# A new order of the work ahead of the loop in a gated cross-attention kernel, with the SiLU table loaded by an instruction of its own

## What is computed

```
x = x + tanh(g_xattn[0]) * L0_xattn(layernorm(x), ctx)      # softmax(q k^T) applied to x
x = x + tanh(g_ffn[0])   * L0_ffn(layernorm(x))             # 256 -> 2 x 704 -> 256
x = x + tanh(g_xattn[1]) * L1_xattn(layernorm(x), ctx)      # 16 heads of 128
x = x + tanh(g_ffn[1])   * L1_ffn(layernorm(x))             # 64 experts, top 8, and a shared one
```

```
def bit_linear(x, w, g):                       # activations to 8 bits, weights to -1, 0, 1
    xn = x * rsqrt(mean(x * x) + 1e-5) * g
    s = 127 / max(|xn|);   xq = round(xn * s) / s
    return xq @ wq.T
gate, up = split(bit_linear(x, gate_w, g1))
return bit_linear(gate * sigmoid(gate) * up, down_w, g2)
```

## Time and profile before

| | |
|---|---|
| median of 3 runs | 617.92 us (616.35 to 618.05) |
| profiled execution | 618.08 us |
| its span in the trace | 616.3 us |
| PE busy | 603.2 us (98%), 3637 matmuls |
| DVE busy | 479.2 us (78%) |
| ACT busy | 422.3 us (69%) |
| POOL busy | 236.1 us (38%); eight to nine tenths in slices 2 to 7 of 40, six or less behind them |
| granted clock of PE | nine tenths or more of full speed in all 40 slices |

### The profile page before, as it was taken

How to read it: one execution, slowest core, us unless ns; L and a number is a source line. 1 busy time by engine, 2 the same in 40 slices (tenths; PEclk the granted TensorE clock), 3 DMA queues, 4 the chain that set the end, 5 groups by cost and what they waited for, 6 DMA issues and landing times.

```text
span 616.3 us, 11599 instructions
## 1 busy us (share of the span) xinstructions
PE 603.2 (98%) x3637; PEld 523.1 (85%) x3637; DVE 479.2 (78%) x1139; ACT 422.3 (69%) x1080; POOL 236.1 (38%) x280
## 2 busy tenths in 40 slices
PE   8889999999999999999999999999999999999997
PEld 6657899999999999999998888888887888887886
DVE  4899889887778687688775787788777677777776
ACT  6998999888888888889898344465444444443442
POOL 5989898666665666556662020000000000000000
PEclk9999999999999999999999999999999999999999
DMA  8423211000000000000030545452956466544540
GB/s 295 147 78 103 82 49 49 31 1 3 1 2 2 2 2 2 1 2 1 11 120 2 157 153 161 128 165 88 226 156 168 116 173 174 157 153 149 196 128 34
DMA packets 33654, 56.47 MB, mean 92 GB/s; under 512 B 12801, under 2 KB 13505, under 8 KB 33601
## 3 DMA queue, kind: packets, MB, share of 16 engines
q1 hardware_dynamic: 33312, 55.82, 29.9%
q10 hardware_dynamic: 288, 0.00, 0.0%
HBM read 53.45 MB, written 1.31 MB: 89 GB/s over the span
## 4 chain that ended last, share of the span: by engine, by line
PE 85%; POOL 4%; DVE 4%; issue 3%; ACT 3%; DMA 1%; SPq 0%; DVEq 0%; ACTq 0%; POOLq 0%
PE bank L298 24%; PE bank L300 24%; PE bank L299 24%; PE bank L967 4%; PE bank L942 2%; PE bank L934 2%; POOL att L584 1%; PE bank L887 1%; DMA wqk<-in_qk 1%; ACT w L1457 1%; PE bank L867 1%; PE bank L814 1%; PE bank L1008 1%; PE bank L801 1%; POOL rk L566 1%
## 5 line engine op out<-in xcount | busy, mean ns | idle before, releaser
L1603 ACT ACTIVATE inter_hi<-inter 128x512 fp32r<-128x512 f32 x63 | 39.8, 632 | 140.6 <-DVE inter L2266 140.6
L298 PE MATMUL bank<-xnT_hi,front_hi 128*128 128x512 f32 (+1 forms) x260 | 102.0, 392 | 0.0
L300 PE MATMUL bank<-xnT_hi,front_lo 128*128 128x512 f32 (+1 forms) x260 | 101.8, 391 | 0.0
L299 PE MATMUL bank<-xnT_lo,front_hi 128*128 128x512 f32 (+1 forms) x260 | 101.7, 391 | 0.0
L2270 DVE TENSOR_TENSOR inter_lo<-inter,inter_hi 128x512 fp32r<-128x512 f32 x63 | 43.6, 692 | 37.9 <-ACT inter_hi L1603 37.3
L1555 ACT ACTIVATE att<-bank,shift,rq 128x256 f32<-128x256 f32 x128 | 71.4, 573 | 0.3 <-DVE shift L2156 0.2
L584 POOL TENSOR_TENSOR att<-att,rowinv 128x512 f32<-128x512 f32 x60 | 63.5, 1074 | 10.6 <-DVE rowinv L2166 10.4
L2239 DVE TENSOR_TENSOR prod<-gate_s,bank 128x512 f32<-128x512 f32 x63 | 43.3, 687 | 21.8 <-PE bank L300 19.7
L566 POOL TENSOR_TENSOR rk<-msq,minus_half 128x4 f32<-128x4 f32 x32 | 33.1, 1035 | 67.9 <-DVE msq L2138 67.7
L2149 DVE TENSOR_REDUCE rowmax<-bank 128x2 f32<-128x512 f32 x64 | 43.7, 685 | 19.2 <-PE bank L300 18.9
L300 PEld LDWEIGHTS bank<-xnT_hi,front_lo 128*128 128x128 f32 x260 | 48.8, 188 | 11.4
(11 more groups left out here) (272 smaller groups left out, 1814.6 us busy)
## 6 DMA issues: line engine op xcount, KB each, us to landing
w_all<-w_rows SPq DMA_DIRECT2D x128, 128.0 KB, 3.0
raw<-in_expert_w SPq DMA_DIRECT2D x32, 384.0 KB, 3.6
wvo_raw<-in_expert_w SPq DMA_DIRECT2D x16, 384.0 KB, 3.6
e_more<-in_expert_w SPq DMA_DIRECT2D x16, 384.0 KB, 3.6
raw<-in_head_qk SPq DMA_DIRECT2D x8, 384.0 KB, 3.7
wvo_raw<-in_head_vo SPq DMA_DIRECT2D x4, 384.0 KB, 3.1
w_keep<-in_head_vo SPq DMA_DIRECT2D x4, 384.0 KB, 3.3
gate_raw<-in_gate_wT SPq DMA_DIRECT2D x2, 704.0 KB, 9.0
```

Source lines behind the costliest of these rows:

```text
L298: pe.matmul(out, l_hi, r_hi_, start=start, stop=False, skip_group_check=True)
L299: pe.matmul(out, l_hi, r_lo_, start=False, stop=False, skip_group_check=True)
L300: return pe.matmul(out, l_lo, r_hi_, start=False, stop=stop, skip_group_check=True)
L1603: act.activation(inter_hi[:, slot, :], inter[:, slot, :], ACT.Copy).then_inc(a_Ihi, 1)
```

## The change

The four lists ahead of the loop are replaced: the same calls stand in them in another order and in part with other PSUM banks, and the bare waits between PE's calls follow the banks. Not only the order differs:

- `load_table(ACT.Silu)` stands directly ahead of `silu_0(0)`, and no longer behind `copy_q2(1, 4)`.
- PE's `keep_busy(1, 7)` became `keep_busy(3, 7)`, and `keep_busy(0, 4)` is new ahead of `gate_0(4)`.

The functions that the lists call, the loop and everything behind it are the same. The core of the diff, with most of the four lists left out (DVE's wholly: its calls keep nearly their places, `scales_1(3)` still behind `absmax_2(3)`):

```diff
             normalise_0(6)
+            normalise_0(7)
             scale_gain(g2, l_g2)
-            normalise_0(7)
+            limit_1(1)
             times_gain(0)
             root_1(2)
-            limit_1(1)
             power_1(2)
             times_gain(1)
+            root_2(0)
             scale_back_1(2)
-            root_2(0)
-            limit_1(2)
             power_2(0)
             low_ctx()
             times_gain(2)
+            limit_1(2)
+            root_1(3)
             rms_k(0)
+            scale_back_2(0)
+            times_gain(3)
             root_2(1)
-            root_1(3)
-            scale_back_2(0)
             power_1(3)
-            times_gain(3)
...
-            keep_busy(1, 7)
-            turn_q1(0, 1)
+            turn_att(2, 2)
+            pe.wait_ge(v_xA, 1)
+            keep_busy(3, 7)
+            turn_q1(0, 3)
...
+            pe.wait_ge(a_s1, 4)
+            keep_busy(0, 4)
             gate_0(4)
...
             split_w(0)
+            copy_att(2, 2)
             turn_gate(1)
-            copy_q1(0, 1)
-            copy_att(2, 5)
+            copy_q1(0, 3)
             copy_rows_0(2, 2)
+            load_table(ACT.Silu)
             silu_0(0)
...
             copy_q2(1, 4)
-            load_table(ACT.Silu)
+            high_m(1, 7)
             square_h(4)
```

More of the change, by code:

```diff
@@ L1125, in _ @@
+            pe.wait_ge(a_Mhi, 3)
+            up_0(6)
             turn_q2(2, 4)
-            pe.wait_ge(a_q1, 8)
-            up_0(6)
-            turn_k(0, 6)
             gate_0(7)
+            up_0(7)
             pe.wait_ge(a_q2, 3)
-            fuse_vo(3, 5)
+            down(2, 5)
             turn_rows_1(0, 4)
-            up_0(7)
-            down(2, 7)
             pe.wait_ge(a_s1, 8)
-            turn_q2(3, 0)
+            turn_k(0, 1)
+            proj_k(2, 0, True)
             pe.wait_ge(a_Mhi, 4)
-            proj_k(2, 5, True)
@@ L1139, in _ @@
-            proj_q(0, 3, True)
+            turn_q2(3, 6)
+            pe.wait_ge(v_h1, 8)
+            fuse_vo(4, 3)
+            proj_q(0, 5, True)
             pe.wait_ge(a_rawK, 3)
-            fuse_vo(4, 5)
-            pe.wait_ge(a_q2, 4)
-            down(3, 1)
-            turn_q(0, 0)
+            fuse_vo(5, 0)
+            down(3, 4)
             pe.wait_ge(v_Klo, 1)
-            fuse_vo(5, 6)
-            pe.wait_ge(a_sqQ, 4)
-            turn_q2(4, 2)
+            turn_q(0, 1)
+            turn_q2(4, 6)
@@ L1149, in _ @@
             pe.wait_ge(a_Mhi, 5)
-            proj_q(1, 5, True)
-            turn_k(1, 4)
+            proj_q(1, 3, True)
             pe.wait_ge(a_Mhi, 6)
+            turn_k(1, 0)
+            pe.wait_ge(a_q2, 5)
             turn_q2(5, 6)
-            proj_k(3, 1, True)
-            pe.wait_ge(a_q2, 5)
-            down(4, 2)
-            turn_q(1, 3)
+            proj_k(3, 2, True)
+            fuse_vo(6, 5)
             pe.wait_ge(a_q2, 6)
             turn_q2(6, 6)
-            pe.wait_ge(a_rawK, 4)
@@ L1161, in _ @@
-            fuse_vo(6, 1)
-            pe.wait_ge(v_Klo, 2)
-            down(5, 4)
+            down(4, 4)
+            scores(0)
+            pe.wait_ge(a_Mhi, 7)
+            down(5, 5)
             pe.wait_ge(a_q2, 7)
             turn_q2(7, 6)
-            pe.wait_ge(a_Mhi, 7)
-            scores(0)
-            turn_k(2, 5)
+            turn_q(1, 3)
+            pe.wait_ge(v_xB, 5)
+            turn_k(2, 4)
+            proj_q(2, 2, True)
+            pe.wait_ge(v_xB, 6)
+            proj_k(4, 5, True)
@@ L1725, in _ @@
-            split_w(4)
-            whole_m(5, 6)
-            copy_q2(4, 2)
-            high_k(1, 4)
-            raw_q(1, 5)
+            whole_m(4, 3)
+            square_q(0, 5)
+            whole_m(5, 0)
+            copy_q2(4, 6)
+            high_q(0, 1)
+            raw_q(1, 3)
+            high_k(1, 0)
             copy_q2(5, 6)
-            raw_k(3, 1)
-            square_q(1, 5)
+            raw_k(3, 2)
+            square_q(1, 3)
+            whole_m(6, 5)
             copy_q2(6, 6)
-            whole_m(6, 1)
+            load_table(ACT.Exp)
```

632 lines of the change are left out of this document (307 added, 325 removed).

## The result

The changed kernel takes 617.88 us (median of 14 runs, 617.28 to 620.17), the kernel before, run beside it, 616.71 us (14 runs, 615.95 to 618.24): a ratio of 1.002, 95% interval 1.001 to 1.0029. The forecast was 615.9 us, faster. The difference lies under the 0.3% that the prediction called tellable, but the interval leaves out 1: in these runs the changed kernel is the slower one.

The account below looks back on a forecast made before the run. PE, busy 98% of the span, was taken as the bound, with some 7 us of waits left ahead of 51.2 us. 618.08 - 2.3 + 0.3 = 616.1 us, or 615.9 us against the median; range 613.7 to 618.8 us.

Parts of the forecast that it names:

- The base: Starting time of the sum: the profiled execution of the kernel before, 618.08 us, 0.16 us above the median of 617.92 us.
- (a): SiLU table load on ACT placed behind the copy of rows: silu_0(0) 0.8 us earlier, counted within (b).
- (b): New POOL order ahead of the joint, limit_1(1) ahead of times_gain(0): scales_1(3) at 45.7 us, 2.3 us earlier.
- the joint: Start of gate_0(6) on PE, behind which matmul follows matmul: 51.46 us before, about 49.2 us forecast.
- (c): Four more keep_busy matmuls ahead of gate_0(4) on PE: about 1.0 us, covered by a 1.9 us wait, costing nothing.
- (d): Stretch behind the joint: POOL's normalise_att(0, 0) comes late for PE's turn(0, 0), so 0.3 us are given back.
- Rival 1: The lead is lost behind the joint, PE idling 1 to 2 us there: 617.1 us, chance 0.22.
- Rival 3: Slower: limit_1(2) on POOL comes too late for silu_0(4) on ACT, 620.1 us; chance 0.12.
- The forecast's own sign of failure: Forecast wrong if the joint comes later than 50.5 us or PE idles over 1 us between it and the loop.

Follow-up runs that it names:

- b_table: Kernel before with one move, load_table(ACT.Silu) directly ahead of silu_0(0): 617.77 us, ratio 1.0021.
- b_rk: Kernel before with b_table's move, limit_1(1) ahead of times_gain(0), power_1(3) behind times_gain(3), root_2(1) and times_rk(0) reordered: 616.59 us, ratio 0.9983.
- b_r7w: b_rk with round_1(7) directly behind times_up_0(5) on VectorE and gate_0(6) waiting for add_down(1): 616.84 us, ratio 0.9997.
- a_again: The changed kernel, unchanged, run again later: 617.78 us, ratio 1.0008 to the kernel before.
- b_same: The kernel before, unchanged, run again for its spread and a second profile: 616.64 us, ratio 0.9996.
- a_same: The changed kernel, unchanged, run again for a second profile: 617.75 us, ratio 1.001 to the kernel before.

## Why the prediction was wrong

**The base.** "The sum is made against the profiled execution, 618.08 us ... it stands 0.16 us above the median of 617.92 us." This step failed, and with it the price of (a) and (b). The three runs shown, 616.35, 617.92 and 618.05 us, came from two courses, and the profile is of the longer. On the shorter one the way from gate_0(0) to gate_0(6) is 1.8 us shorter (27.08 against 25.31 us) without any change. That is the 0.93 us for SiLU, of which (a) counted 0.8 us, and most of the 1.29 us that (b) counted for limit_1(1): most of the 2.3 us was there already in the runs of the shorter course.

**(a)** Held as a mechanism: the load starts 0.02 us behind the copy of rows, limit_1(0) is no condition for it, and its end starts the next activation; there is no drain of 1.38 us as by the Trainium skill (ScalarE: Activation LUTs, What ACT_TABLE_LOAD costs). As a gain it exists only on the longer course. Alone it is a loss of 1.2 us (b_table), by the hold of limit_1(1) that the prediction had named for that operation's new place, not for this step.

**(b)** limit_1(1) took 0.40 us (0.30 forecast), root_1(2) came without idling, scales_1(3) without a wait. From gate_0(0) to gate_0(6) the changed kernel takes 23.99 us, 3.1 us less than the profile of the prediction; 0.5 us of it is lost ahead of gate_0(0), 16.05 against 15.54 us, which no step named. With the start taken out, gate_0(6) comes 2.6 us earlier, where 2.3 us was forecast. But the end of times_gain(3) is not what sets the joint, as the prediction argued: in b_rk it and scales_1(3) come earlier and the joint does not. The place of round_1(7) on VectorE, which no step named, is worth 0.75 us (b_r7w). Which parts of the lists bring the other 0.9 us (24.90 to 23.99 us) was not tried.

**(c)** Right: covered, with 0.68 us to spare.

**(d)** The second step that failed, by its size: "0.3 us are given back", measured 2.15 us (95.39 against 93.24 us). normalise_att(0, 0) was late for turn(0, 0) as described, by 0.55 us. power_3(1) took its 0.7 us, but both_w(5), forecast 1.3 us earlier, came only 0.4 us earlier counted from the first energy matmul (62.61 against 63.05 us), as TensorE, whose turn_q2 it waits for, had by then lost time at turn_rows_1(0). Two waits were not seen: normalise_1(0) behind times_gain(5), 0.77 us, and values(1), 0.51 us, behind a mean_q(3) that took 2.96 us beside low_w and normalise_att of POOL. The three make 1.83 us, the waits of the old order in that stretch 0.55 us. That leaves 0.9 us of the 2.15 us, most of it only a matter of counting: the idle time in brackets begins at the modelled end of the matmul ahead, which runs on into the gap, and the shortest gaps are not printed. Counted from start to start, beyond the usual spacing of such a matmul, the delays over 0.15 us sum to 3.05 us in six places, against 1.10 us in three of the old order: 1.95 us of the 2.15 us.

**The rivals.** Rival 1, "the lead is lost behind the joint", is what happened, more strongly than it was priced: of a lead of 2.6 us at the joint 2.15 us are gone by scores(9), and against the shorter course the lead had been 0.8 us only. Its ground, that lists without slack lose a lead, is not what the runs show; the losses are single waits that the new order of POOL and VectorE made. Rival 3 did not occur: silu_0(4) at 43.56 us follows its neighbour without idling, limit_1(2) had ended at 42.84 us, 0.7 us ahead. The forecast's own sign of failure, more than 1 us of TensorE idling behind the joint, is in the profile; so is rival 1's, a joint near 49 us (48.89 us in a_again).

The numbers then close: against the shorter course (b_same, 134.02 us) the changed kernel takes 135.4 us, 1.4 us more, beside 1.1 us between a_same and b_same in the medians; against the longer one (135.9 us) 0.5 us less, where 2.0 us was forecast. The kernel before is a mixture of both, in shares that differ from one set of runs to the next, on one chip too: over 617.5 us are 6 of 14 runs in the result and, beside the runs here, 10 of 34, 12 of 35 and later 16 of 29 on the same chip, 16 of 29, 11 of 17 and 6 of 17, some of which may be late starts. How the changed kernel compares with its median follows that share.

## What to carry to other kernels

Before a sum is made against a profile, compare its time with each single run: where they fall in heaps, take a second profile, because waits of the longer course are no price that a change can win. Where GpSimd and VectorE work on small and large tiles side by side, a short operation on the path can cost five times its time by an offset of less than 0.1 us (1.59 against 0.33 us here); take it out of the neighbourhood of two-input operations rather than count on it. A lead that all engines share is kept through a stage where TensorE is busy to within 0.2 us (1.8 us here); one that comes with a new order of POOL and VectorE has to be followed through that stage operation by operation, as one new wait or hold there takes it back.

## What the hardware showed beyond expectation

A small VectorE operation was held just as a GpSimd one was: 2.96 us instead of 0.17 us for four numbers (mean_q(3)), across four GpSimd instructions in a row (two normalise_att, two low_w), while VectorE's operations with an input in PSUM on both sides of it took their usual 0.7 us.

The first eight matmuls, of 512 columns each, took 3.67 to 5.96 us in the profiles (3.73, 4.59 and 5.96 us in three executions of the changed kernel), which moves the whole span by up to 2.3 us. The difference is one of clock: in the profile with 5.96 us they start 0.85 us apart up to the sixth (0.99 us after the first) and 0.43 us apart at the end, and 0.43 to 0.85 is the step from 2.4 to 1.2 GHz, the two levels of the granted clock. The windows print a clock of 1.00 for that stretch, but the trace's own record of the full clock begins at 10.20 us only; in a_again the matmuls are 0.43 us apart from the second on, and that record begins at 5.45 us. In a_warm, with eleven warm-up matmuls, the eight took 4.00 us but started 0.5 us later, at 5.99 us, so nothing came of it. Why the full clock comes later in some executions no run here shows.
